# Self attention scores: the mask matmul replaced by a bias in the exponential and a select on GpSimd

## What is computed

```python
x = _layernorm(tgt, ln1_g, ln1_b)
q, k, v = (_heads(t) for t in jnp.split(x @ sa_wqkv, 3, axis=-1))
wei = jnp.einsum('bhtd,bhsd->bhts', q, k) * scale
wei = jnp.where(causal[None, None], wei, NEG_INF)
wei = jnp.where(tgt_padding_mask[:, None, None, :], NEG_INF, wei)
wei = jax.nn.softmax(wei, axis=-1)
result = tgt + _merge(jnp.einsum('bhts,bhsd->bhtd', wei, v)) @ sa_wproj + sa_bproj
# then cross attention over src (375 rows, no mask), added to result,
# and relu(_layernorm(tgt) @ ff_w1 + ff_b1) @ ff_w2 + ff_b2, added to result
```

## Time and profile before

| what | value |
|---|---|
| time, median of 3 runs | 676.9 us (673.03 to 678.33) |
| the profiled execution: time, span | 671.41 us, 669.5 us |
| PE busy | 590.5 us (88%), 5564 instructions |
| DVE busy | 415.0 us (62%) |
| ACT busy | 326.9 us (49%) |
| POOL busy | 128.6 us (19%), 370 instructions |
| chain that ended last, by engine | PE 49%, DVE 15%, SP's queue 13%, DMA 10%, ACT 7%, issue 3%, POOL 2% |

### The profile page before, as it was taken

One profiled execution on the slowest core, in us unless ns is written; L12 is line 12 of the kernel. 1 busy time (PEld: TensorE's weight loads), 2 busy tenths in 40 slices (PEclk: granted clock), 3 DMA queues, 4 the chain that ended last, 5 costly groups with the idle time before them and its releaser, 6 DMA issues.

```text
span 669.5 us, 14170 instructions
## 1 busy us (share of the span) xinstructions
PE 590.5 (88%) x5564; PEld 447.6 (67%) x5564; DVE 415.0 (62%) x982; ACT 326.9 (49%) x613; POOL 128.6 (19%) x370
## 2 busy tenths in 40 slices
PE   3497797699999998699999998899999999999696
PEld 3385576576777776576777776676777777767564
DVE  5984563678557644678557644678557644685371
ACT  2133453336635655346635655346635655365064
POOL 6701310203003210203003211103003211130010
PEclk9966998799999999799999999699999999999798
DMA  8294049176560049176570048176570057005700
GB/s 234 75 132 85 1 86 143 41 93 74 107 126 24 10 92 141 43 96 73 107 125 23 12 95 143 36 96 75 109 125 19 11 93 129 24 2 103 92 2 15
DMA packets 73122, 52.08 MB, mean 78 GB/s; under 512 B 21920, under 2 KB 72288, under 8 KB 73056
## 3 DMA queue, kind: packets, MB, share of 16 engines
q1 hardware_dynamic: 73056, 51.17, 46.0%
HBM read 14.36 MB, written 1.84 MB: 24 GB/s over the span
## 4 chain that ended last, share of the span: by engine, by line
PE 49%; DVE 15%; SPq 13%; DMA 10%; ACT 7%; issue 3%; POOL 2%; DVEq 0%; POOLq 0%; ACTq 0%
SPq L532 12%; PE misc L1068 9%; DMA tb<-in_x 6%; PE pvb L1039 6%; PE scb L1023 6%; PE mxb L1007 5%; PE misc L925 5%; DVE negm L837 5%; PE misc L927 4%; PE misc L926 4%; PE misc L1075 4%; DMA k2st<-kp 2%; DVE rem L771 2%; ACT prob L708 2%; PE misc L1046 1%
## 5 line engine op out<-in xcount | busy, mean ns | idle before, releaser
L708 ACT ACTIVATE prob<-scb 125x448 f32<-125x448 f32 (+1 forms) x256 | 137.5, 543 | 74.3 <-PE scb L1023 68.7
L837 DVE TENSOR_REDUCE negm<-mxb 112x1 f32<-112x375 f32 x256 | 130.4, 540 | 25.2 <-PE mxb L1007 23.4
L1039 PE MATMUL pvb<-prob,v 125*17 125x112 f32 (+1 forms) x2048 | 96.4, 266 | 0.3 <-ACT ot L715 0.3
L1007 PE MATMUL mxb<-k2st,q2st 96*112 96x375 bf16 x256 | 87.1, 356 | 2.4 <-DVE negm L837 1.6
L1023 PE MATMUL scb<-q2st,k2st 128*125 128x112 bf16 x768 | 78.5, 225 | 0.2
L1023 PEld LDWEIGHTS scb<-q2st,k2st 128*125 128x125 bf16 x768 | 66.3, 137 | 16.9 <-issue 8.8
L627 POOL CAST mparts<-negm 112x8 bf16<-112x8 f32 x64 | 12.2, 191 | 333.4 <-DVE negm L837 175.4
L834 DVE TENSOR_REDUCE negm<-mxb 112x4 f32<-112x448 f32 x64 | 39.6, 619 | 43.8 <-PE mxb L1004 43.6
L1068 PE MATMUL misc<-wf,hT 128*112 128x256 f32 x256 | 60.9, 386 | 3.2 <-DVE rem L771 3.2
L1039 PEld LDWEIGHTS pvb<-prob,v 125*17 125x17 f32 (+1 forms) x2048 | 35.0, 95 | 35.8 <-issue 21.7
L1068 PEld LDWEIGHTS misc<-wf,hT 128*112 128x112 f32 x256 | 44.9, 179 | 14.6 <-DVE rem L771 4.8
(11 more groups left out here) (153 smaller groups left out, 1238.2 us busy)
## 6 DMA issues: line engine op xcount, KB each, us to landing
k2st<-kp SPq DMA_DIRECT2D x192, 93.8 KB, 4.3
xs<-in_ctx SPq DMA_DIRECT2D x16, 375.0 KB
q1st<-qp SPq DMA_DIRECT2D x48, 112.0 KB, 5.6
k1st<-kp SPq DMA_DIRECT2D x48, 112.0 KB, 7.0
q2st<-qp SPq DMA_DIRECT2D x96, 56.0 KB, 2.3
xn<-in_x SPq DMA_DIRECT2D x4, 448.0 KB, 12.2
tb<-in_x SPq DMA_DIRECT2D x8, 224.0 KB, 10.0
out<-ostage SPq DMA_DIRECT2D x16, 112.0 KB, 3.3
```

The lines of the kernel that those rows point to most:

```text
L708: nc.scalar.activation(prob[0:rows, n % PROB_SLOTS, :], scb[n % SCORE_BANKS][0:rows, 0:GH * T], ACT.Exp, scale=SCALE).then_inc(s_ex, 1)
L837: V.tensor_reduce(negm[:, at, i:i + 1], mx[0:T, 0:S], axis=AX_X, op=ALU.max, negate=True).then_inc(s_mx, 1)
L1007: mm = M(mx[0:T, 0:S], q2st[0:NROW, i, b * T:(b + 1) * T], k2st[k2_place(q, b)][0:NROW, i, 0:S], start=True, stop=True)
L1039: mm = M(pvb[32 * j:32 * j + VW, g * T:(g + 1) * T], vals, prob[0:rows, slot, j * T:(j + 1) * T], start=(c == 0), stop=(c == chunks(u) - 1))
```

## The change

The scores of the self units lose their mask matmul. What it did is done in two other places. The padding of a key is added by ACT as the exponential's bias, a column of `pad` with one value per partition (keys are on the partitions there). The keys later than the query are set to zero in `prob` by POOL, with one affine_select over 112 partitions by 448 elements for each of the 64 self scores. pv of a self unit now waits for this select (`s_sel`) where it waited for the exponential (`s_ex`). The maxima keep their mask matmul and `maskt`. Since the scores no longer read `maskt`, the step that rebuilds it waits for the last maximum of the group before in place of the last score.

```diff
--- before.py
+++ after.py
@@ -372,6 +372,7 @@
         s_xh = sem("xq_hi_made")
         s_xs = [sem(f"src_landed{i}") for i in range(2)]
         s_pad = sem("pad_terms_made")
+        s_sel = sem("later_keys_cleared")
         s_mask = sem("mask_tile_made")
         s_bn = sem("row_stats_made")
         s_mv = sem("mean_var_made")
@@ -432,6 +433,7 @@
         signalled(s_resb, od.of("norm2"))
         for s in (s_pad, s_mask):
             signalled(s, od.of("mask"))
+        signalled(s_sel, [t for t in scores if t[2] < BG])
         for m in range(KT):
             for b in range(BG):
                 signalled(s_k2st[b][m], [t for t in od.of("stack_k2") if t[2:] == (b, m)], LAND)
@@ -616,6 +618,12 @@
                     after(pool, s_tb[h], ("load_tb", s[1], h))
                     nc.gpsimd.tensor_tensor(tb[:, 2 * h:2 * h + 2, :], tb[:, 2 * h:2 * h + 2, :],
                                             sab[:, :].unsqueeze(1).broadcast_to([T, 2, C]), ALU.add).then_inc(s_res, 1)
+                elif kind == "score" and s[2] < BG:
+
+                    after(pool, s_ex, s)
+                    p = prob[0:T, scores.index(s) % PROB_SLOTS, :].rearrange("p (h t) -> p h t", h=GH)
+                    nc.gpsimd.affine_select(out=p, in_=p, compare_op=ALU.is_ge, fill=0.0,
+                                            base=0, pattern=[[0, GH], [1, T]], channel_multiplier=-1).then_inc(s_sel, 1)
                 elif kind == "max_parts":
 
                     q, u, half = s[1:]
@@ -705,8 +713,10 @@
                     after(act, s_sc, s)
                     prev = before_in(scores, s, PROB_SLOTS)
                     after(act, s_pv, prev and ("pv",) + prev[1:])
+
+                    bias = pad[:, q * BG + s[2]:q * BG + s[2] + 1] if s[2] < BG else 0.0
                     nc.scalar.activation(prob[0:rows, n % PROB_SLOTS, :], scb[n % SCORE_BANKS][0:rows, 0:GH * T], ACT.Exp,
-                                         scale=SCALE).then_inc(s_ex, 1)
+                                         bias=bias, scale=SCALE).then_inc(s_ex, 1)
                 elif kind == "ot":
                     u = s[2]
                     after(act, s_pv, ("pv", q, u, 3, chunks(u) - 1))
@@ -784,7 +794,7 @@
                 if kind == "mask":
                     V.tensor_copy(padneg[:, :], pad[:, q * BG:(q + 1) * BG]).then_inc(s_pad, 1)
                     after(dve, s_pad, s)
-                    after(dve, s_sc, ("score", q - 1, BG - 1, 3, 0) if q else None)
+                    after(dve, s_mxf, ("max", q - 1, BG - 1, 3) if q else None)
                     for b in range(BG):
                         i = V.tensor_scalar(maskt[:, b, :], causal[:, :], padneg[:, b:b + 1], None, ALU.add)
                     i.then_inc(s_mask, 1)
@@ -1014,13 +1024,10 @@
                     sc = scb[scores.index(s) % SCORE_BANKS]
                     after(pe, s_ex, before_in(scores, s, SCORE_BANKS))
                     after(pe, s_read["act"], ("mT", q, u, g // 2))
-                    if u < BG:
-                        M(sc[0:T, 0:GH * T].rearrange("p (h t) -> p h t", h=GH), identb[0:T, :],
-                          maskt[:, b, :].unsqueeze(1).broadcast_to([T, GH, T]), start=True, stop=False)
                     for j in range(GH):
                         h = g * GH + j
                         ks = k1st[:, h, b * T:(b + 1) * T] if u < BG else k2st[k2_place(q, b)][:, h, c * SC:(c + 1) * SC]
-                        mm = M(sc[0:rows, j * T:(j + 1) * T], ks, (q1st if u < BG else q2st)[:, h, b * T:(b + 1) * T], start=(u >= BG), stop=(u >= BG or j == GH - 1))
+                        mm = M(sc[0:rows, j * T:(j + 1) * T], ks, (q1st if u < BG else q2st)[:, h, b * T:(b + 1) * T], start=True, stop=True)
                     mm.then_inc(s_sc, 1)
                 elif kind == "pv":
 
@@ -1030,7 +1037,7 @@
                         prev = unit_before(q, u)
                         after(pe, s_ot, prev and ("ot", *prev))
                     after(pe, s_read["act"], ("v1", q, b) if u < BG else ("v2", q, b, 2))
-                    after(pe, s_ex, ("score", q, u, g, c))
+                    after(pe, s_sel if u < BG else s_ex, ("score", q, u, g, c))
                     slot = scores.index(("score", q, u, g, c)) % PROB_SLOTS
                     rows = T if u < BG else SC
                     for j in range(GH):
```

## The result

The changed kernel takes 683.9 us in the median (677.1 to 686.7, 20 runs), the kernel before 674.0 us (667.7 to 678.3, 20 runs). The ratio is 1.0155, 95% interval 1.0132 to 1.0178, or +10.4 us (8.9 to 12.0) where +0.2 was forecast. It ends inside the range of 670.5 to 684.5 and outside "within 1%". The profiled executions have spans of 682.2 and 669.5 us, 12.7 apart. The first lines of the page of the changed kernel answer to the earlier trace rows; the PEclk line is the granted clock in 40 slices.

The account below looks back on a forecast made before the run. The prediction took PE to be bound by its waits for POOL behind the `tb` load; -7.0 (removal) + 5.1 (behind resid) + 1.6 (start) + 0.3 (bias) + 0.2 (group 3) = +0.2 us, median 677.1 us, range 670.5 to 684.5.

Parts of the forecast that it names:

- What bounds the kernel: PE is busiest, but its long waits in groups 0 to 2 follow POOL's resid, which waits for the `tb` load.
- The removal: Mask matmuls gone from self scores: 33 of the 64, on the path outside the start, save 7.0 us.
- the bias: Self exponentials on ACT take 92 ns more each; one ahead of the load in groups 0 to 2 costs +0.3 us.
- The select's price: Each of 64 selects on POOL takes 0.57 us, with bounds of 0.29 and 1.27 us.
- The rival of the dear select: Selects on POOL take 1.11 or 1.27 us each, giving 682.5 or 684.1 us; chance 0.18.
- Behind resid: Selects (2, 2) and (2, 3) queue on POOL behind resid: +1.7 us in each of groups 0 to 2, +5.1 us.
- The start: Units 0 and 1 of group 0: added latencies make pv (1, 2) 1.6 us later, removed mask matmuls already counted.
- I cost them at nothing: Selects of units 0 and 1 in groups 1 to 3 have enough slack, tightest 1.73 us at (1, 0): no cost.
- The clock: PE's half clock behind the load waits may shorten or lengthen: taken as no change, with bounds of +-5 us.
- the clock decides: Rival: 672 us if half clock falls into PE's longer pause, 682 if it lasts longer in each group; chance 0.10 each.

## Why the prediction was wrong, step by step

The parts were priced well; what failed is what was put at nothing. The sum added the removal and the select as if neither changed the other, took no cost for the clock, and took none for the selects of units 0 and 1 in groups 1 to 3. The runs showed +3.3 us in place of -7.0 for the removal beside the select, some 12 us more of half clock, and 3.3 us at one of those quarters, where a load landed 2.3 us later than before.

**What bounds the kernel** was right: PE waits, at few places, for what POOL does behind a load. Moving those two steps took 1.9% off the kernel before.

**The removal**, -7.0 us, and **the bias**, +0.3, were right by themselves: -5.7 us for both (interval -8.2 to -3.1). The bias alone, +1.0 us with an interval from -1.3 to +3.3, is not told from nothing. The step that failed is that this value was carried into the sum with the select. Beside the select the removal was worth +3.3.

**The select's price** was right, 592 ns against 570, inside the bounds of 0.29 and 1.27. The rival of the dear select, which needed 1.11 or 1.27 us, falls. The time did come out near its 682.5 and 684.1, by another way.

**Behind resid**, +1.7 us in each of three groups: the mechanism stood as forecast, in order and in what ends the pause. The measured jumps are 3.9, 2.3 and 0.6 us, 6.8 in place of 5.1. In group 2 the kernel before had 10.2 us of half clock behind the wait (the earlier trace rows shows a part) and the changed one 6.8, in group 1 it was the other way round; that this makes the one jump small and the other large is likely, and no run shows it. In group 0 the load landed 16.8 us behind its issue, before 14.1; the kernel with the select alone has 16.5, the one without select 14.2. No term of the sum had a later landing. mT came 7.0 us behind the landing in group 1 (277.25 to 284.22), 5.5 to 6 were forecast.

**The start**, +1.6 us: pv (1, 2) came 1.3 later, a little better than forecast:

```profile
66.97 0.39 PE L1046 MATMUL pvb<-prob,v 112*17 112x112 f32 x8 [0.84 <-POOL prob L625]
...
72.23 0.58 PE L1046 MATMUL pvb<-prob,v 112*17 112x112 f32 x8 [0.35 <-POOL prob L625]
...
76.36 0.39 PE L1046 MATMUL pvb<-prob,v 112*17 112x112 f32 x8
```

But PE was at half clock by then (0.58 us for the pv at 72.23, 0.39 at 70.95 in the earlier trace rows), and pv (1, 3) came 2.8 later. In the kernel with the start's mask matmuls back, at full clock, it came 1.4 later. The sum looked one row too short and did not ask for the clock here.

**"I cost them at nothing"**, the units 0 and 1 of groups 1 to 3, is a step that failed. It looked at (1, 0), 1.73 us from exponential to pv, and took it for the tightest. It is quarter (1, 2), whose select stands behind the first resid; by slack of exponential and pv it looked roomy, by POOL's order it depends on a load. With the landing of the kernel before it would have been roomy still: there resid ended at 204.77, a select behind it would end at 205.4, and pv (1, 2) ran at 206.18. The load took 5.6 us in place of 3.3, and that made it 3.3 us in group 1, 1.7 of pause and 1.6 at half clock behind it. In group 2, with 3.4 us, it cost nothing, in group 3, with 4.5, 0.6. The 2.0 us of (0, 2) in group 2 were at nothing too; there PE waited for copies, not for a select.

**The clock**, "I take neither, and +-5 us", is the main failure. The mean granted clock went from 0.951 to 0.943, from 65.6 to 77.8 us at half clock, 12.2 more and up to 6.1 us of time. The bound had the right size. Taking the middle of it was wrong: in the start both edits push the same way, as one takes work from PE where it is short of it and the other adds pauses, and only the kernels with both had half clock there. In the other places that is argued, not shown. And it was looked for only behind the known waits, where the low level lasted 6.8, 10.2 and 6.8 us, against 6.8, 6.8 and 10.2 before; new were the start, 215 and 352 us, 13.7 us together. The rival "the clock decides", 682 and chance 0.10, was the nearest, with its place wrong. That 683.9 lies inside the stated range is luck: the range was laid around 677.1, from a median of 676.9 before, and that of the 20 runs is 674.0.

What stays open: how the 10 us between the halves divide. The time at half clock differs by enough for up to 8.4 us between the two kernels with selects, whose spans differ by 4.4; loads that land 1 to 3 us later are in it too, and a pause behind such a load is followed by half clock, so that the two are not independent. Only in the start is the clock's share shown nearly alone: from pv (1, 2) to pv (1, 3) the changed kernel takes 4.1 us at half clock, and with the mask matmuls back 2.6. No run held the clock or the landings fixed elsewhere. Why the copies ahead of the load took longer in the changed kernel is not known either.

## What to carry to other kernels

Price two halves of a change together when both take work from the same engine at the same place: each total was right to 1.0 us here, and their sum was wrong by 9. On an engine that runs in program order, slack is not only the gap from producer to consumer; list for each added instruction what stands ahead of it in its own queue, and which of these wait for a load (here those of quarters (1, 2), (2, 2) and (2, 3)), and ask what happens if that load lands two microseconds later. Moving such a waiting step behind the next user was worth 1.9%, more than any arithmetic in this change.

## What was not expected of the hardware

Removing 64 matmuls of 0.19 us can cost time. Beside the selects, with them the clock stayed at 1.00 from 68 to 76 and 214 to 222 us, without them it was 0.57 and 0.79, and the program with more work was 3.3 us faster, give or take 2.8. Eight of them, 1.5 us of PE's work, gave 5 us back. And a load of 224 KB, issued at the same 206.9 us of the same program part, took 3.4 us or 5.6 us to land; the DMA engines had been busy for 0.36 or 0.52 of the four microseconds ahead of it. A pause of PE of 1.8 us and a stretch of half clock hung on that.
